# A graph network's node accumulator kept transposed, and one float32 product of its edge network in three half-precision products

## What is computed

```python
h  = relu(layernorm(x))                                   # per node
e  = relu(ea @ ee_w1 + ee_b1) @ ee_w2 + ee_b2             # per edge (and per self loop, ea = 0)
agg = segment_sum(h[src] + e, dst)                        # edges and self loops
h0 = (1 + eps) * h + agg
h1 = relu(ln(h0 @ w1 + b1)); h2 = relu(ln(h1 @ w2 + b2))  # 256 -> 1024 -> 1024
x  = x + relu(ln(h + h2 @ w3 + b3))                       # 1024 -> 256
```

## Time and profile before

| | us |
|---|---|
| median of 3 runs | 3159.29 (3156.21 to 3159.81) |
| span of the profiled execution | 3157.3 |
| its own time beside the span | not given apart from the three runs |
| TensorE matmuls busy | 2446.9 (77%) |
| VectorE busy | 2156.6 (68%) |
| GpSimd busy | 1976.9 (63%) |
| ScalarE busy | 1488.6 (47%) |

### The profile page before, as it was taken

How to read it: one execution, slowest core, us unless ns; L and a number is a source line. 1 busy time by engine, 2 the same in 40 slices (tenths; PEclk the granted TensorE clock), 3 DMA queues, 4 the chain that set the end, 5 groups by cost and what they waited for, 6 DMA issues and landing times. The chain is left out here.

```text
span 3157.3 us, 79016 instructions
## 1 busy us (share of the span) xinstructions
PE 2446.9 (77%) x25310; PEld 2164.9 (69%) x25311; DVE 2156.6 (68%) x3833; ACT 1488.6 (47%) x3803; POOL 1976.9 (63%) x2143
## 2 busy tenths in 40 slices
PE   0577777777777789999999999947777777777763
PEld 0466666666666679999999999945555555555552
DVE  7676667777677636666666666657766766666666
ACT  5444444444444458888888888831111111111114
POOL 4677777777777634444444444437777777777772
PEclk9998889999899889999999999978888888887996
DMA  6555555555555500000000000026555655555554
GB/s 158 168 161 149 158 154 166 161 163 160 159 164 158 143 25 18 21 21 20 20 21 20 20 22 21 21 61 178 171 173 173 174 172 168 173 172 173 171 170 136
DMA packets 183839, 373.69 MB, mean 118 GB/s; under 512 B 42598, under 2 KB 93688, under 8 KB 183769
## 3 DMA queue, kind: packets, MB, share of 16 engines
q0 software_dynamic: 75552, 209.66, 23.5%
q1 hardware_dynamic: 107392, 162.37, 17.4%
q10 hardware_dynamic: 824, 0.87, 0.1%
HBM read 346.95 MB, written 25.80 MB: 118 GB/s over the span
## 5 line engine op out<-in xcount | busy, mean ns | idle before, releaser
L446 POOL DMA_INDIRECT rows<-tab_scratch,srcs x784 | 765.7, 977 | 238.7 <-issue 234.1
L1458 POOL DMA_INDIRECT a_rows<-tab_scratch,srcs x784 | 750.5, 957 | 251.7 <-issue 235.8
L1524 PE MATMUL sum_ps<-feat,a_hot 128*125 128x264 f32 x1960 | 601.5, 463 | 237.5 <-DVE feat L1616 121.0
L1524 PEld LDWEIGHTS sum_ps<-feat,a_hot 128*125 128x125 f32 x1960 | 417.4, 222 | 341.7 <-DVE feat L1616 133.9
L876 PE MATMUL z_ps<-ah,w 128*128 128x125 f16 x6400 | 553.8, 219 | 1.0 <-PEq L982 1.0
L876 PE MATMUL z_ps<-al,w 128*128 128x125 f16 x3200 | 542.7, 217 | 0.0
L876 PEld LDWEIGHTS z_ps<-ah,w 128*128 128x128 f16 x6400 | 489.5, 97 | 1.5 <-issue 1.4
L1468 ACT ACTIVATE feat<-d 128x32 f32<-128x32 f32 x196 | 44.9, 229 | 827.0 <-DVE d L1612 566.2
L500 PE MATMUL mlp_ps<-ewa,eab 128*128 128x256 f16 x788 | 203.5, 290 | 284.3 <-PEq L496 283.3
L478 ACT ACTIVATE rh<-mlp_ps 128x1024 f16<-128x1024 f32 x196 | 199.7, 1019 | 358.2 <-ACTq L477 347.7
L829 POOL TENSOR_TENSOR a<-a 128x500 f32<-128x500 f32 x100 | 124.4, 1244 | 372.1 <-POOLq L828 372.1
(11 more groups left out here) (211 smaller groups left out, 5422.8 us busy)
## 6 DMA issues: line engine op xcount, KB each, us to landing
ea<-edge_t SPq DMA_DIRECT2D x394, 128.0 KB
dstb<-dst_flat SPq DMA_DIRECT2D x98, 512.0 KB
rows<-tab_scratch,srcs POOLq DMA_INDIRECT x784
a_rows<-tab_scratch,srcs POOLq DMA_INDIRECT x784
tab_scratch<-prow SPq DMA_DIRECT2D x50, 128.9 KB
hx<-x SPq DMA_DIRECT2D x50, 125.0 KB
x_scratch<-x SPq DMA_DIRECT2D x50, 125.0 KB
hs<-tab_scratch SPq DMA_DIRECT2D x50, 125.0 KB
```

What stands on the lines that cost most here:

```text
L446: pool.indirect_dma_start(rows[:, b % DEEP, k, :], None, dram["tab0"], bass.IndirectOffsetOnAxis(ap=srcs[:, c:c + 1], axis=0),).then_inc(r ...
L1458: pool.indirect_dma_start(rows[:, b % DEEP, k, :], None, dram["tab1"], bass.IndirectOffsetOnAxis(ap=srcs[:, c:c + 1], axis=0),).then_inc(r ...
L1524: ins = pe.matmul(out[:], hot[:, h, k, :], feat[:, row, k, :], start=(k == 0), stop=(k == CB - 1))
```

## The change

The accumulator is kept transposed: in each tile's 512 columns stand four pieces of 128 (feature on the partition, node in the column, 125 of 128 used). `sums` swaps its operands: the gathered rows and activations are stationary, the one-hot matrix moves. So nothing has to be turned in `nodes`. In exchange `prepare` has to bring the own term in transposed, by TensorE from the table's halves. The bias `ee_b1` of the self loops is put into `acc` at the fill. In `nodes` the product with `ee_w2` is made like the others.

```diff
 prepare, GpSimd (ScalarE fills the other half in the same way)
-            pool.memset(acc[:, 0:NT // 2, D:2 * D], 0.0)
+            pool.wait_ge(ld_ecol, 16)
+            for j in range(KD):
+                pool.tensor_scalar(accT[:, 0:NT // 2, KD + j, :], ecol[:, 0, j:j + 1]...broadcast_to([P, NT // 2, P]), 0.0, None, ALU.max)
 prepare, ScalarE
+            def own(c):
+                act.wait_ge(own_done, c + 1)
+                act.activation(accT[:, tiles(c), 0, 0:TN], own_ps[c % 2][0][:, 0:PG, 0:TN], ACT.Identity,
+                               bias=own_off[:, 0:1], scale=eps2[:]).then_inc(own_kept[0], 1)
-            for c in range(CH + 2):
-                if c >= 2:
+            for c in range(CH + 3):
+                if c >= 3:
+                    own(c - 3)
+                if 2 <= c < CH + 2:
                     high(c - 2)
 prepare, TensorE (new)
+            for c in range(CH):
+                pe.wait_ge(tb_ready, c + 1)
...
+                for k in range(PG):
+                    for j in range(KD):
+                        out = own_ps[c % 2][j][:, k, 0:TN]
+                        pe.matmul(out, tb[:, c % 2, k, j * P:(j + 1) * P], ident16[0:TN, 0:TN], start=True, stop=False)
+                        ins = pe.matmul(out, tb[:, c % 2, k, D + j * P:D + (j + 1) * P], ident16[0:TN, 0:TN], start=False, stop=True)
+                ins.then_inc(own_done, 1)
 prepare, VectorE
             def own(c):
-                h = acc[0:TN, tiles(c), 0:D]
-                dve.wait_ge(t_ready, c + 1)
-                settled(dve.scalar_tensor_tensor(out=h, in0=h, scalar=eps1[0:TN, :], in1=ht[:, c % 2], op0=ALU.mult, op1=ALU.add))
+                dve.wait_ge(own_done, c + 1)
+                dve.tensor_scalar(accT[:, tiles(c), 1, 0:TN], own_ps[c % 2][1][:, 0:PG, 0:TN], eps2[:], own_off[:, 1:2],
+                                  ALU.mult, ALU.add).then_inc(own_kept[1], 1)
 edges0, TensorE
-                    lhs = hot[:, h, k, :]
-                    pe.matmul(out[:, 0:D], lhs, rows[:, ring, k, 0:D], ...)
-                    pe.matmul(out[:, 0:D], lhs, rows[:, ring, k, D:2 * D], ...)
-                    pe.matmul(out[:, D:2 * D], lhs, rh[:, s, k, :], ...)
-                    ins = pe.matmul(out[:, D:2 * D], lhs, rl[:, s, k, :], ...)
+                    rhs = hot[:, h, k, :]
+                    for q in range(2 * KD):
...
+                        to = out[:, q, 0:TN]
+                        pe.matmul(to, high, rhs, start=(k == 0 and q == 0), stop=False, skip_group_check=True)
+                        ins = pe.matmul(to, low, rhs, start=False, stop=(k == CB - 1), skip_group_check=True)
 nodes, TensorE
+            def make_h(i):
+                pe.wait_ge(e_split, 1)
...
                 for j in range(KD):
                     f = slice(j * P, (j + 1) * P)
-                    pe.matmul(h_ps[:, j, :], w2e[:, 0, f], rt[:, 0, :], start=True, stop=False)
-                    own = pe.matmul(h_ps[:, j, :], ur[:, p, f], ident[0:TN, 0:TN], start=False, stop=False)
...
-                    ins = pe.matmul(h_ps[:, j, :], w2e[:, 1, f], rt[:, 1, :], start=False, stop=True)
+                    ins = products(h_ps[:, j, :], lambda k: eh[:, k, :], lambda k: el[:, k, :],
+                                   lambda k: w2e16[:, k, 0, f], lambda k: w2e16[:, k, 1, f], KD)
                 ins.then_inc(h_done, 1)
 nodes, TensorE, body
                 if has(i, 0):
                     variance(0)
+                if has(i, 0, 1):
+                    make_h(i + 1)
                 if has(i, 1):
                     layer2(1, range(1, 4), 1 - p)
...
-                    output(range(FIRST))
-                if has(i, 0, 1):
-                    make_h(i + 1, 1 - p)
-                if has(i, 0, 2):
-                    turn(i + 2, p)
-                if has(i, 2):
-                    output(range(FIRST, KH)).then_inc(y_done, 1)
+                    output(range(KH)).then_inc(y_done, 1)
 nodes, ScalarE
             def high_h():
-                act.activation(hh[:], h_ps, ACT.Copy, scale=1.0 / WS).then_inc(hh_ready, 1)
+                act.activation(hh[:], h32[:], ACT.Copy, scale=1.0 / WS).then_inc(hh_ready, 1)
+            def high_e(i):
+                r = accT[:, bass.ds(i, 1), KD:2 * KD, 0:TN].rearrange("p a q n -> p (a q) n")
+                act.activation(eh[:], r, ACT.Copy, scale=1.0 / WS).then_inc(eh_ready, 1)
             def body(i, p):
                 if has(i, 0, 1):
-                    turned(i + 1)
+                    high_e(i + 1)
 nodes, VectorE (low_e: after row_norm(0); whole_h: after row_norm(1), ahead of squares)
+            def whole_h(i):
+                dve.wait_ge(h_done, 1)
...
+                dve.tensor_tensor(h32[:], h_ps[:], a_own, ALU.add).then_inc(h_ready, 1)
+            def low_e(i):
+                dve.wait_ge(eh_ready, 1)
...
+                dve.scalar_tensor_tensor(out=el[:], in0=r, scalar=1.0 / WS, in1=eh[:], op0=ALU.mult, op1=ALU.subtract).then_inc(e_split, 1)
```

More of the change, by code:

```diff
@@ L142, in prepare @@
         spans_sb = m.sb("spans_sb", [half, 2, 2], I32)
+        own_ps = [[m.ps(f"own{s}{j}_ps", [P, 8, P]) for j in range(KD)] for s in range(2)]
         ld_x = [m.sem(f"ld_x{c}") for c in range(CH)]
@@ L151, in prepare @@
         tb_ready, t_free = m.sem("tb_ready"), m.sem("t_free")
+        ld_ecol, own_coef, own_done = m.sem("ld_ecol"), m.sem("own_coef"), m.sem("own_done")
+        own_kept = [m.sem(f"own_kept{j}") for j in range(KD)]
         tb_stored = [m.sem(f"tb_stored{s}") for s in range(2)]
@@ L292, in _ @@
             dve.wait_ge(ld_small, 16 * 6)
+            dve.wait_ge(ld_ecol, 16)
             settled(dve.tensor_scalar(eps1[:], eps1[:], 1.0, None, ALU.add))
+            dve.tensor_scalar(own_off[:], ecol[:, 1, :], eps1[:], -1.0, ALU.mult, ALU.mult)
+            dve.tensor_copy(ident16[:], sb["ident"][:])
+            settled(dve.tensor_scalar(eps2[:], eps1[:], 1.0, None, ALU.add))
+            dve.sem_inc(own_coef, 1)
             settled(dve.tensor_copy(sb["ewa"][:], er[:]))
@@ L305, in _ @@
             dve.tensor_copy(spans_sb[:], sched_sb[:].rearrange("p c j -> p j c")).then_inc(sched_ready, 1)
-            for c in range(CH + 2):
-                if c >= 2:
+            for c in range(CH + 3):
+                if 2 <= c < CH + 2:
                     low(c - 2)
-                if 1 <= c < CH:
-                    own(c - 1)
+                if c >= 3:
+                    own(c - 3)
                 if c + 1 < CH:
@@ L314, in _ @@
                     coefficients(c + 1)
-            own(CH - 1)
+            for j in range(KD):
+                dve.wait_ge(own_kept[j], CH)
     return range(m.sems[0].num, m.sems[-1].num + 1)
@@ L505, in sums @@
                 for k in range(CB):
-                    lhs = hot[:, h, k, :]
-                    pe.matmul(out[:, 0:D], lhs, rows[:, ring, k, 0:D], start=(k == 0), stop=False, skip_group_check=True)
-                    pe.matmul(out[:, 0:D], lhs, rows[:, ring, k, D:2 * D], start=False, stop=False, skip_group_check=True)
-                    pe.matmul(out[:, D:2 * D], lhs, rh[:, s, k, :], start=False, stop=False, skip_group_check=True)
-                    ins = pe.matmul(out[:, D:2 * D], lhs, rl[:, s, k, :], start=False, stop=(k == CB - 1), skip_group_check=True)
+                    rhs = hot[:, h, k, :]
+                    for q in range(2 * KD):
+                        r = slice(q % KD * P, (q % KD + 1) * P)
+                        if q < KD:
+                            high, low = rows[:, ring, k, r], rows[:, ring, k, D + q * P:D + (q + 1) * P]
+                        else:
+                            high, low = rh[:, s, k, r], rl[:, s, k, r]
+                        to = out[:, q, 0:TN]
+                        pe.matmul(to, high, rhs, start=(k == 0 and q == 0), stop=False, skip_group_check=True)
+                        ins = pe.matmul(to, low, rhs, start=False, stop=(k == CB - 1), skip_group_check=True)
                 return ins
@@ L942, in scores @@
                 ins.then_inc(att_done, 1)
-            turn(0, 0)
             bias_sums()
-            pe.wait_ge(ld_w2e, 16)
-            pe.wait_ge(rt_ready, 1)
-            pe.sem_inc(rt_ready, -1)
-            make_h(0, 0)
-            turn(1, 1)
+            pe.wait_ge(w2e_split, 1)
+            make_h(0)
             def body(i, p):
@@ L1123, in _ @@
             dve.memset(ones[:], 1.0 / H).then_inc(ones_ready, 1)
-            dve.sem_inc(v1_read, 1)
+            dve.wait_ge(ld_w2e, 16)
+            settled(dve.tensor_scalar(w2e16[:, :, 0, :], w2e[:], WS, None, ALU.mult))
+            settled(dve.scalar_tensor_tensor(out=w2e16[:, :, 1, :], in0=w2e[:], scalar=WS, in1=w2e16[:, :, 0, :],
+                                             op0=ALU.mult, op1=ALU.subtract))
+            dve.sem_inc(w2e_split, 1)
+            dve.sem_inc(v_read, 1)
             dve.sem_inc(x1_stored, 16)
@@ L1230, in body @@
```

(6 more changed lines are left out.)

120 lines of the change are left out of this document (60 added, 60 removed).

## The result

The changed kernel takes **3195.9 us** (median of 4, 3192.7 to 3200.8), the kernel before 3159.6 beside it: a ratio of 1.0116, 95% interval 1.0102 to 1.0130. The forecast was 3166.6 with a range up to 3179.

A forecast was written before the change was run, and what follows sets the result against it. Bounds: preparation by a ring of small waits, edge stage by GpSimd's gathers, node stage by TensorE, then a loop of waits. +6.3 (preparation) + 0 (edges) + 1 (nodes) = +7.3 us on the span, giving 3166.6 us, range 3157 to 3179.

The forecast's parts named there:

- First edge stage, 0: First edge stage: doubled matmuls in sums cost TensorE 10 us more, covered by GpSimd's gathers, so no change.
- The node stage's loop: Node stage: waits from layer 2's end through activations, high, low to next layer 2; 7.34 plus layer 2's 11.67 makes 19.01.
- The other edits ride under this loop: Node stage: changed passes on ScalarE, VectorE (two of 250, about 0.42 us each) and GpSimd cost no time.
- The node stage's start, +0.5 and +1.5: Node stage: w2e's split before the first tile costs +0.5 us; make_h's 0.67 paid in the first passes costs +1.5.
- Preparation, +6.3: Preparation: +0.9 us from slower chunks (6.8 us each) and +5.4 from a longer tail (19.3 us).
- Earlier, the first stores hold ScalarE up, which hides a later start: Preparation before 46 us: ScalarE already waits for the first stores, so a later start was given no price.
- with ScalarE's and GpSimd's opening fills late as well: +10: Preparation: upper bound of its change, +10 us, if both engines' opening fills also come late.
- A: Node stage: the loop is not in charge, TensorE's 0.88 us is gained on 44 tiles; 3128 us, chance 0.10.
- C: Node stage, layer 2: make_h's products come slower, at 0.08 us pitch +13 us, total 3179.5; chance 0.17.
- B: Preparation: transposes are done before ScalarE wants them, +0 to +1 us, total 3161; chance 0.15.
- D: Node stage: new waits let the granted clock fall, +22 us, total 3189; chance 0.04 given with E.
- E: First edge stage: doubled matmuls make TensorE slower than the gathers' 5.12 us per block; chance 0.04 given with D.

The follow-up runs named there:

- both edits: The changed kernel with h kept in the accumulator (high_h and low_h read h_ps) and make_h's products put behind the whole second layer: 3142.7 us, 0.9947 of the kernel before.

## Why the prediction was wrong, point by point

- **First edge stage, 0:** right (-0.5). The distance between starts in `sums` is 0.056 us (599.78, 599.84, 599.90, 599.95), and GpSimd's gathers set the pace.
- **The node stage's loop:** right. 7.34 + 11.67 = 19.01 was forecast, 7.36 + 11.66 was measured as soon as low_h no longer stood in its way, and 18.40 without `make_h` inside, for a forecast of 18.34. TensorE's own 18.15 (18.14 above) and the twelve products' 0.67 (1568.45 to 1569.12) fit too.
- **"The other edits ride under this loop":** this is the step that failed. Its "about 0.42 each" prices VectorE's two new passes, and they held (0.41 each). But low_h, an old pass of which the change moves an operand, got no price at all: it was left at its 0.42, and the chain that it stands in was never added up. That chain, from layer 2's end over `high_h`, `low_h` and layer 1 to the next layer 2, needs 7.10 us with a pass of 0.42 and 7.76 with 1.08. The loop needs 7.34. So the chain was 0.24 from taking charge, and by these sums the longer pass costs 0.42 a tile; measured, it is 0.40 (19.43 for 19.03 with h in the accumulator). 45 tiles at 0.40 are 18.0 of the 27.4 us.
- **Why 1.08.** The edit moved one operand of low_h from PSUM to SBUF, at a moment when GpSimd folds squares. The profile of before held the warning, in passes of other names. The same normalisation of 125x256 elements took 0.41 at one place and 1.11 at the other, and GpSimd was folding at the second only, until 1518.32; the pass ended at 1518.46. The two work on different data (`x` and `hx`), but in the three tiles in which the second met no GpSimd instruction it took 0.41 too.

```profile
1507.46 0.41 DVE L1195 TENSOR_SCALAR h<-x,mv,rrow 125x256 f32<-125x256 f32 x1 [0.15 <-DVEq L1121]
...
1517.35 1.11 DVE L1195 TENSOR_SCALAR hx<-hx,mv,rrow 125x256 f32<-125x256 f32 x1 [0.15 <-DVEq L1121]
```

```profile
1517.07 1.25 POOL L829 TENSOR_TENSOR a<-a 128x500 f32<-128x500 f32 x1 [4.18 <-POOLq L828]
```

A pass with two tensors in SBUF, as low_h has them now, stood there as well. It took 1.63 where GpSimd had begun an add ahead of it, and 1.20 where not. (The short row is the same pass of the other layer; the long one took 1.20 too in the two tiles where no add was under way.)

```profile
1504.73 1.45 POOL L851 TENSOR_TENSOR hx<-hx,bpack 125x256 f32<-125x256 f32 x1 [2.48 <-POOLq L850]
1505.61 1.63 DVE L1184 TENSOR_TENSOR z<-z,rstd 128x1000 f32<-128x1000 f32 x1
...
1515.92 1.20 DVE L1184 TENSOR_TENSOR z<-z,rstd 128x1000 f32<-128x1000 f32 x1
```

The Trainium skill says it outright ("SBUF — State Buffer", Who interferes with whom): a VectorE instruction with two SBUF inputs contends with a GpSimd instruction that reads SBUF, and the one that comes second is blocked until the first is done. The runs agree for low_h: 0.42 with one operand in PSUM beside the fold, 0.42 with both in SBUF and no fold, otherwise an end 0.28 us behind GpSimd's. The normalisation above and the casts of the preparation have one tensor operand, so this sentence doesn't speak of them; for them only the rows do. The prediction weighed another rule and not this one.
- **The node stage's start, +0.5 and +1.5:** too small. Up to the fifth low_h the stage loses 9.1 us: 2.1 to the first low_h (9.84 for 7.77 from the stage's start), 2.6 to the second, 4.5 over the next three. But the second's share isn't the change's: the node stage of before took 14.80 us from first to second low_h in one run and 17.12 in the run with only the fill changed. Part of the rest may be the clock: from about 22 to 42 us behind the stage's start it was granted 1.00 before (1130 to 1150) and 0.75 after (1142 to 1162). With both edits the three tiles take 56.1 in one run and 59.1 in another, so this start spreads by 3 us by itself. How the remainder splits wasn't tested.
- **Preparation, +6.3; measured +12.0.** The chunk of 6.8 was 6.68, the transposes came 0.104 us apart for a forecast of 0.103, ScalarE waited 1.32 for a forecast of 1.6, its `own` took 0.88 for an estimate of 0.68, and the tail of 19.3 was 18.3: +4.4 for +5.4. The failed step is the sentence "Earlier, the first stores hold ScalarE up, which hides a later start". The start was 9.9 us late and only 2.4 of it had been won back by the tenth normalisation. What could hide it was one wait for the first store, which made one interval of the kernel before 9.40 us instead of 6.63 (36.56 to 45.96), so 2.8 at most:

```profile
43.93 1.27 ACT L229 ACTIVATE tb<-ht 125x1280 f16<-125x1280 f32 x1 [4.80 <-DMA tab_scratch<-tb]
```

The bound "with ScalarE's and GpSimd's opening fills late as well: +10" named the place, but the forecast took the fill's price as nothing. 16.57 us for two fills of 3200 where one memset of 6400 took 5.46 could not be known from the rows; that VectorE stands behind GpSimd's fill could, since a first cast of 128x125 had taken 6.18 us there beside the memset (GpSimd to 7.79, the cast to 7.87; in the changed kernel, with no fill beside it yet, it took 0.23):

```profile
1.69 6.18 DVE L255 CAST iota<-icol 128x125 f16<-128x125 int32 x1 [0.81 <-POOL ithr L193]
...
2.33 5.46 POOL L195 MEMSET acc<- 128x6400 f32 x1
```

- **The rest, 0; measured +2.6.** Its program isn't changed, and over the runs it is 1040.0 to 1046.0 us.
- **The rivals.** A was the other side of the result: TensorE's 0.88 a tile is there, and with h in the accumulator and `make_h` behind layer 2 the node stage is 26.2 us shorter than before. C, whose own total of 3179.5 lay just outside the range, had the mechanism ("any lengthening of the loop counts in full from the first nanosecond") and the wrong place and size: the products come 0.056 us apart, and it was the leg beside the loop that grew. B, D and E fell: ScalarE waited for the transposes, the clock stayed at 1.00 in the middle of the stage, and GpSimd hardly waited.

## What to carry to other kernels

Where an edit moves an operand between PSUM and SBUF, its pass gets a new price that depends on what GpSimd does at that moment: look in the trace for two passes of one shape and two durations, and see whether the longer one ends with a GpSimd instruction. A gap of 0.24 us between two chains is not cover: when one loop is found to be in charge, add up the next one too, with every duration that the edit touches. And put new work outside the leg that closes the loop; here two lines moved and one operand left in the accumulator turned +1.2% into -0.5%, and a later `own` into -0.9%.

## What the runs showed of the hardware

- A VectorE pass that is held up by a GpSimd instruction in SBUF shows no wait in the profile; it shows a longer duration. A cast of 128x50 read 16.95 us, one of 128x256 8.07, and the casts, the normalisation and low_h (250 elements) ended 0.06 to 0.28 us behind GpSimd's instruction. `z<-z,rstd`, with 1000 elements, ended 1.06 behind, so with two tensors in SBUF what follows the hold grew with the size of the pass.
- It goes the other way too. In the kernel before, GpSimd's add to `hx` (125x256) took 0.72 us in the one tile where it met no VectorE pass, but 1.45 in nearly all others, where it started 0.3 us behind VectorE's `al<-a,ah` (1504.42 to 1505.60). Which of the two came first can't always be read from the starts: the two long casts at the kernel's start, beside the memset and beside the fill, have starts 0.64 and 0.26 us ahead of GpSimd's. Reductions of 100x512 at 0.69 us ran through beside the fill (5.83 to 9.0) untouched.
- A GpSimd tensor_scalar that fills 128x3200 float32 columns takes 8.3 us, 2.6 ns a column; its memset 0.85 ns; VectorE did such a fill in 1.89 us and ScalarE in 2.9.
- Two GpSimd instructions of 0.2 us each at the kernel's start, with the wait ahead of them, made 784 later gathers 15 to 16 ns shorter in the mean, and the kernel about 10 us faster. Before a small loss is put down to an edit's mechanism, the mean duration of the instruction that sets the pace should be compared.
